# Third layer's experts: all sorted rows kept in SBUF, each tile's outputs scattered from GpSimd into per-token places, plain loads at the end, rank matmuls moved ahead of the projections

## The reference

```python
xn = _layernorm(x, axis=-1)
x = x + _L2_attn_ref(xn, ...) + _L2_ffn_ref(xn, ...)

def _L2_ffn_ref(hidden_states, Wg, W1, W2, W3, bias):      # E = 8, TOP_K = 2, FFN = 128
    x = hidden_states.reshape(-1, hidden_dim)
    routing_weights = jax.nn.sigmoid(x @ Wg.T)
    scores = routing_weights + bias
    _, top_k_index = jax.lax.top_k(scores, TOP_K)
    top_k_weights = jnp.take_along_axis(routing_weights, top_k_index, axis=1)
    top_k_weights = top_k_weights / top_k_weights.sum(axis=-1, keepdims=True)
    expert_w = jnp.einsum('tk,tke->te', top_k_weights, one_hot)
    g = jax.nn.silu(x W1[e]) * (x W3[e]) * expert_w[..., e]
    out = sum over e of g W2[e]
```

## Time and profile before

| | |
|---|---|
| median of 3 runs | 2058.43 us (2058.09 to 2062.5) |
| the profiled execution | 2054.93 us, of which the span is 2053.1 us |
| third layer, from its normalization to its last addition | 656.5 to 806.4 us of the span |
| its loop over 23 tiles of experts | 729.4 to 779.1 us |
| TensorE busy over the span | 90% |
| VectorE, ScalarE, GpSimd busy | 63%, 48%, 52% |

### The profile page before, as it was taken

The page is one execution under the profiler, slowest core; times in us unless marked ns, Lnnn a source line. Parts: engine busy times, 40 slices in busy tenths (PEclk is TensorE's granted clock), DMA queues, the critical chain, the costliest instruction groups (busy, mean ns, idle before and its releaser), DMA issues.

```text
span 2053.1 us, 45861 instructions
## 1 busy us (share of the span) xinstructions
PE 1850.3 (90%) x16855; PEld 1191.3 (58%) x16855; DVE 1287.1 (63%) x2490; ACT 995.4 (48%) x2433; POOL 1072.0 (52%) x2252
## 2 busy tenths in 40 slices
PE   7799997867898885898999999999999999999987
PEld 5422664422244453445677777777777777677766
DVE  2544564685577422535777777777777777777753
ACT  2375232215321341434566656655665666566653
POOL 0521222323100302033888888887888878888873
PEclk7899999989999796899999999999999999999999
DMA  6044422200001333101222222222222222222221
GB/s 155 1 121 148 109 46 56 72 34 1 20 25 26 96 106 95 34 19 40 53 55 61 55 52 63 63 54 53 63 63 54 53 58 63 53 53 62 44 53 33
DMA packets 229260, 121.36 MB, mean 59 GB/s; under 512 B 141712, under 2 KB 208816, under 8 KB 228784
## 3 DMA queue, kind: packets, MB, share of 16 engines
q1 hardware_dynamic: 223424, 109.06, 21.3%
q0 software_dynamic: 5616, 9.38, 2.2%
HBM read 84.88 MB, written 36.68 MB: 59 GB/s over the span
## 4 chain that ended last, share of the span: by engine, by line
PE 22%; POOL 20%; issue 6%; SPq 3%; DVE 3%; DMA 3%; ACT 2%; POOLq 0%; DVEq 0%; ACTq 0%
POOL a_term L2594 8%; POOL a_z L2598 8%; PE ps L2046 5%; PE ps L2056 3%; PE ps L2245 3%; SPq L1979 2%; POOL a_rstd L2570 2%; POOL a_xnorm L2576 2%; DMA a_l<-a_v_dram 2%; PE ps L2276 2%; SPq L1987 1%; DVE a_v L2653 1%; PE ps L2212 1%; PE ps L2286 1%; PE ps L2221 1%
## 5 line engine op out<-in xcount | busy, mean ns | idle before, releaser
L2594 POOL TENSOR_TENSOR a_term<-a_z,a_l 32x14 f32<-32x14 f32 (+6 forms) x896 | 342.1, 382 | 70.3
L2598 POOL TENSOR_TENSOR a_z<-a_z,a_term 32x14 f32<-32x14 f32 (+6 forms) x896 | 341.7, 381 | 70.2
L2624 DVE SCALAR_TENSOR_TENSOR a_qkv<-a_raw,a_taps,a_qkv 128x1024 f32<-128x1024 f32 x192 | 247.0, 1286 | 6.1
L2046 PE MATMUL ps<-all_xn,a_w_qkv 128*128 128x512 f32 x512 | 246.9, 608 | 0.0
L388 POOL DMA_INDIRECT f_rows<-a_row,a_slots x32 | 35.7, 1116 | 192.1 <-DVE a_of_tile L377 146.7
L2245 PE MATMUL ps<-a_out_t,a_w_out 128*128 128x256 f32 x512 | 129.1, 395 | 1.9 <-ACT a_out_t L2468 1.7
L2046 PEld LDWEIGHTS ps<-all_xn,a_w_qkv 128*128 128x128 f32 x512 | 89.1, 193 | 69.3 <-issue 67.5
L2389 ACT ACTIVATE a_raw<-ps 128x512 f32<-128x512 f32 x128 | 76.3, 598 | 108.7 <-PE ps L2046 108.0
L2056 PE MATMUL ps<-a_w_z,all_xn 128*128 128x256 f32 x512 | 122.6, 383 | 0.0
L849 POOL DMA_INDIRECT f_sums<-a_y,a_xs x23 | 36.0, 1566 | 136.5 <-ACT a_y L798 133.5
L2588 POOL COPY a_z<-a_l 32x256 f32<-32x256 f32 x64 | 27.4, 429 | 152.3 <-DMA a_l<-a_v_dram 152.0
(11 more groups left out here) (331 smaller groups left out, 4303.7 us busy)
## 6 DMA issues: line engine op xcount, KB each, us to landing
a_gc_rows<-a_g_dram SPq DMA_DIRECT2D x64, 256.0 KB, 4.7
a_v_dram<-a_v SPq DMA_DIRECT2D x64, 256.0 KB
a_w<-in_f_w SPq DMA_DIRECT2D x24, 512.0 KB, 4.5
a_w_qkv<-in_a_w SPq DMA_DIRECT2D x16, 512.0 KB, 3.8
a_t_dram<-a_z SPq DMA_DIRECT2D x512, 8.0 KB
a_xs<-f_rows SPq DMA_DIRECT2D x46, 130.0 KB, 2.2
a_w_z<-in_a_w SPq DMA_DIRECT2D x16, 256.0 KB, 2.8
a_w_out<-in_a_wo SPq DMA_DIRECT2D x16, 256.0 KB, 3.1
```

The source lines that it names most:

```text
L2046: mm = pe.matmul(ps[:, to, :], w_qkv[:, k, mt * P:(mt + 1) * P], xn[:, k, b * T:(b + 1) * T], start=k == 0, stop=k == KC - 1)
L2594: pool.tensor_tensor(term[:, 0:j, j + 1:], z[:, 0:j, j:j + 1].broadcast_to([HP, j, n]), rows[:, j:j + 1, j + 1:].broadcast_to([HP, j, n]), ...
L2598: pool.tensor_tensor(z[:, 0:j, j + 1:], z[:, 0:j, j + 1:], term[:, 0:j, j + 1:], ALU.add).then_inc(sub_step, 1)
L2624: dve.scalar_tensor_tensor(to, rows, tap, to, ALU.mult, ALU.add).then_inc(conv_ready if j == TAPS - 1 else conv_step, 1)
```

## The change

- All 23 tiles of sorted rows get a place in SBUF (`xs` has `SLOT_TILES` tiles in place of 6). SP loads them in 8 groups right after the scatter, with no wait on the loop.
- The third layer has its own DRAM tensor of rows, which SP fills with blank rows at the end of the loads that it issues in the normalization block. A blank row ends in a place number of its own, past those of the tokens.
- A row ends in its place, `k * N + token`, for the token's choice k. When a tile's `y` is ready GpSimd scatters it with a plain indirect DMA to these places. `y` is a ring of 6 tiles, and ScalarE waits, before it writes a tile again, for that tile's scatter to have landed.
- The stores of `y` by SP and the 16 gathers of GpSimd are gone. SP waits for all scatters and loads the sums with 8 plain DMAs of 256 KB each.
- The rank matmuls stand ahead of the projections.

```diff
@@ class Routing
-    def __init__(self, nc, s, whole, d, name, by_sigmoid, rows=None):
-        self.taken_over = rows is not None
-        self.rows = rows if self.taken_over else nc.dram_tensor(name + "_rows", (SLOT_TILES * P, ROW), F32).ap()
-        self.sums = None if self.taken_over else nc.dram_tensor(name + "_sums", (N + P, C), F32).ap()
+    def __init__(self, nc, s, whole, d, name, by_sigmoid, apart):
+        self.places = TOP * N if apart else N
+        self.rows = nc.dram_tensor(name + "_rows", (SLOT_TILES * P, ROW), F32).ap()
+        self.sums = nc.dram_tensor(name + "_sums", (self.places + (SLOT_TILES if apart else 1) * P, C), F32).ap()
@@ load_rest
-            sp.dma_start(self.row[:, k, :, C + 1:], d["token"]).then_inc(self.r_loaded, 16)
+            sp.dma_start(self.row[:, k, :, C + 1:], d["token"][k if self.apart else 0]).then_inc(self.r_loaded, 16)
@@ fill
+        rows = self.rows.rearrange("(i p) w -> p i w", p=P)
+        if self.apart:
+            sp.dma_start(rows, self.d["blank_apart"]).then_inc(self.filled, 16)
+            return
@@ scatter
-            if not self.taken_over:
-                pool.wait_ge(self.filled, 2 * 16)
+            pool.wait_ge(self.filled, 16 if self.apart else 2 * 16)
@@ linear_and_experts, load
             sp.dma_start(bo[:, :], d["a2_bo"]).then_inc(loaded, 16)
+            route.fill(sp)
@@ buffers
-        XS, DEEP = 6, 3
-        xs, xt = s.buf("xs", [P, XS, ROW]), s.buf("xt", [P, DEEP, KC, P])
+        DEEP, YS = 3, 6
+        xs, xt = s.buf("xs", [P, SLOT_TILES, ROW]), s.buf("xt", [P, DEEP, KC, P])
+        GROUPS = ((0, 1), (1, 2), (2, 4), (4, 7), (7, 11), (11, 15), (15, 19), (19, SLOT_TILES))
-        y, got = s.buf("y", [P, 4, C]), s.buf("got", [P, TOP, TT, C])
+        y, got = s.buf("y", [P, YS, C]), s.buf("got", [P, TOP, TT, C])
@@ SP
                 sp.wait_ge(route.scattered, 16 * TOP * TT)
-                for i in range(XS):
-                    load_rows(i)
-                for i in range(TILES):
-                    store(i)
-                    if i + XS < TILES:
-                        load_rows(i + XS)
+                for n, (a, z) in enumerate(GROUPS):
+                    sp.dma_start(xs[:, a:z, :], route.rows[a * P:z * P, :].rearrange("(i p) w -> p i w", p=P)
+                                 ).then_inc(xs_loaded[n], 16)
+                for v in range(YS):
+                    sp.wait_ge(y_put[v], 16 * ((TILES - 1 - v) // YS + 1))
+                for pair in range(TT // 2):
+                    for k in range(TOP):
+                        first = k * N + 2 * pair * P
+                        sp.dma_start(got[:, k, 2 * pair:2 * pair + 2, :], route.sums[first:first + 2 * P, :].rearrange(
+                            "(t p) c -> p t c", p=P)).then_inc(got_loaded[pair], 16)
@@ TensorE
                     route.turn_rows(pe, ps, ROW_BANK + p % 2, xn, ident, p)
+                route.ranks(pe, ps, ROUTE_BANK)
                 pe.wait_ge(loaded, 4 * 16)
                 for t in range(NT):
...
-                    if t == 3:
-                        route.ranks(pe, ps, ROUTE_BANK)
@@ ScalarE, take_y
-                    if i >= 4:
-                        act.wait_ge(y_stored[i % 4], 16 * (i // 4))
-                    act.activation(y[:, i % 4, :], ps[:, Y[i % 2], 0:C], ACT.Copy,
-                                   scale=xs[:, i % XS, C:C + 1]).then_inc(y_ready, 1)
+                    if i >= YS:
+                        act.wait_ge(y_put[i % YS], 16 * (i // YS))
+                    act.activation(y[:, i % YS, :], ps[:, Y[i % 2], 0:C], ACT.Copy,
+                                   scale=xs[:, i, C:C + 1]).then_inc(y_ready, 1)
@@ GpSimd
-                for v in range(4):
-                    pool.wait_ge(y_stored[v], 16 * ((TILES - 1 - v) // 4 + 1))
-                for tt in range(TT):
-                    for k in range(TOP):
-                        pool.indirect_dma_start(got[:, k, tt, :], None, y_dram, bass.IndirectOffsetOnAxis(
-                            route.slots[:, k, tt:tt + 1], 0)).then_inc(got_loaded[tt // 2], 16)
+                for i in range(TILES):
+                    pool.wait_ge(y_ready, i + 1)
+                    pool.indirect_dma_start(
+                        route.sums, bass.IndirectOffsetOnAxis(xs[:, i, C + 1:C + 2].bitcast(U32), 0),
+                        y[:, i % YS, :], None).then_inc(y_put[i % YS], 16)
@@ VectorE
-                    dve.wait_ge(got_loaded[pair], 16 * TOP * 2)
+                    dve.wait_ge(got_loaded[pair], 16 * TOP)
```

More of the change, by code:

```diff
@@ L186 @@
 class Routing:
[L190 to L195 removed]
+    def __init__(self, nc, s, whole, d, name, by_sigmoid, apart):
+        self.name, self.d, self.by_sigmoid, self.apart = name, d, by_sigmoid, apart
+        self.places = TOP * N if apart else N
+        self.rows = nc.dram_tensor(name + "_rows", (SLOT_TILES * P, ROW), F32).ap()
+        self.sums = nc.dram_tensor(name + "_sums", (self.places + (SLOT_TILES if apart else 1) * P, C), F32).ap()
         self.wr = s.buf("wr", [P, KC, E_ALL])
@@ L243, in fill @@
     def fill(self, sp):
-        sp.dma_start(self.rows.rearrange("(i p) w -> p i w", p=P),
-                     self.d["blank"].unsqueeze(1).broadcast_to([P, SLOT_TILES, ROW])).then_inc(self.filled, 16)
+        rows = self.rows.rearrange("(i p) w -> p i w", p=P)
+        if self.apart:
+            sp.dma_start(rows, self.d["blank_apart"]).then_inc(self.filled, 16)
+            return
+        sp.dma_start(rows, self.d["blank"].unsqueeze(1).broadcast_to([P, SLOT_TILES, ROW])).then_inc(self.filled, 16)
         sp.dma_start(self.sums.rearrange("(i p) w -> p i w", p=P),
@@ L403, in rope_and_experts @@
     with Stage(nc, "a0") as s:
-        route = Routing(nc, s, whole, d, "f0", False)
-        rows = route.rows
+        route = Routing(nc, s, whole, d, "f0", False, False)
         FF = 512
@@ L1303, in _, with linear_and_experts @@
                                                  ALU.add, ALU.add).then_inc(added, 1)
-def linear_and_experts(nc, whole, ps, d, x, xn, ident, norm, rows):
+def linear_and_experts(nc, whole, ps, d, x, xn, ident, norm):
     with Stage(nc, "a2") as s:
@@ L1313, in linear_and_experts @@
         wo, bias, bo = s.buf("wo", [P, KC, C]), s.buf("bias", [P, 3, KC]), s.buf("bo", [P, KC])
-        route = Routing(nc, s, whole, d, "f2", True, rows)
+        route = Routing(nc, s, whole, d, "f2", True, True)
         FF = 128
@@ L1341, in linear_and_experts @@
             s.sem("ctx_ready"), s.sem("out_ready"), s.sem("added"))
-        xs_loaded = [s.sem(f"xs_loaded{v}") for v in range(XS)]
+        xs_loaded = [s.sem(f"xs_loaded{n}") for n in range(len(GROUPS))]
         xt_psum, xt_ready, h_psum, silu_ready, gated_ready, gt_psum, gt_ready, y_psum, y_ready = (
@@ L1345, in linear_and_experts @@
             s.sem("gt_psum"), s.sem("gt_ready"), s.sem("y_psum"), s.sem("y_ready"))
-        y_stored = [s.sem(f"y_stored{v}") for v in range(4)]
-        got_loaded = [whole.sem(f"f2_got_loaded{pair}") for pair in range(TT // 2)]
+        y_put = [whole.sem(f"f2_y_put{v}") for v in range(YS)]
+        got_loaded = [s.sem(f"got_loaded{pair}") for pair in range(TT // 2)]
         both_added, sum_psum, sums_added = s.sem("both_added"), s.sem("sum_psum"), s.sem("sums_added")
@@ L1418, in turn_x @@
                 def turn_x(i):
-                    pe.wait_ge(xs_loaded[i % XS], 16 * (i // XS + 1))
+                    for n, (a, z) in enumerate(GROUPS):
+                        if i == a:
+                            pe.wait_ge(xs_loaded[n], 16)
                     if i >= 2:
@@ L1422, in turn_x @@
                     for k in range(KC):
-                        mm = pe.transpose(ps[:, XT[i % 2], k * P:(k + 1) * P], xs[:, i % XS, k * P:(k + 1) * P],
+                        mm = pe.transpose(ps[:, XT[i % 2], k * P:(k + 1) * P], xs[:, i, k * P:(k + 1) * P],
                                           ident[:, :])
@@ L2923, in _constants @@
         "tile_no": np.tile(np.arange(SLOT_TILES, dtype=f), (P, 1)),
-        "token": _row_ends(np.arange(N).reshape(TT, P).T),
+        "token": np.stack([_row_ends(k * N + np.arange(N).reshape(TT, P).T) for k in range(TOP)]),
         "blank": np.concatenate([np.zeros((P, C + 1), f), _row_ends(N + np.arange(P))], axis=1),
+        "blank_apart": np.concatenate([np.zeros((P, SLOT_TILES, C + 1), f), _row_ends(
+            TOP * N + np.arange(SLOT_TILES * P).reshape(SLOT_TILES, P).T)], axis=2),
     }
@@ L2998, in build @@
         if "a0" in stages:
-            rows = rope_and_experts(nc, s, ps, d, x, xn, ident, looked_up)
+            rope_and_experts(nc, s, ps, d, x, xn, ident, looked_up)
         def norm(name):
@@ L3009, in build @@
         if "a2" in stages:
-            linear_and_experts(nc, s, ps, d, x, xn, ident, norm("n2"), rows)
+            linear_and_experts(nc, s, ps, d, x, xn, ident, norm("n2"))
         if "a3" in stages:
```

9 lines of the change are left out of this document (removed).

## The result

The changed kernel takes 2030.74 us (median of 4 runs, 2026.41 to 2033.46) against 2058.26 us beside it; the ratio is 0.9863, with a 95% interval of 0.9844 to 0.9882. Forecast were 2030.8 us. The total agrees better than its parts do, so the layer has to be taken apart.

The account below looks back on a forecast made before the run. Bounds: TensorE's wait for sorted rows, the loop's 2.19 us pace on a six-tile ring, and a 27.26 us end. Start 3.8, loop 10.3 and end 13.5 sum to 27.6 us off 2058.43: 2030.8 us, range 2025 to 2036.

Parts of the forecast that it names:

- Ranks first: Layer start: rank matmuls ahead of projections bring `place` and first scatter 7.3 us earlier, tile 0's transposes only 2.8 us.
- The clock: Layer start: without an idle stretch TensorE keeps 2.4 GHz through transposes and output matmuls, gaining 1.0 us.
- Resident rows: Third layer's loop: no load hangs on it, outputs come every 1.62 us in place of 2.19, gaining 10.3 us.
- Rival C: Loop keeps its old pace, the first two outputs showing only TensorE's saved-up lead: 2041.1 us, chance 0.07.
- The scatter beside the loop: GpSimd's 23 `y` scatters take 0.97 us plus 0.30 pause, 1.27 a tile against 1.62, so they hide at no cost.
- rivals A and B: Loop scatters: GpSimd becomes the bound at 1.86 us a tile (chance 0.10), or VectorE shuts it out at 2.27 (0.05).
- The end: Last `y` to last addition: 8 plain loads replace the gathers, 13.8 us in place of 27.26, gaining 13.5.
- the bound of 10.8 from 247 GB/s: Final loads' pessimistic case: 2.10 MB at 247 GB/s plus 2.3 us, 10.8 us in place of 7.9, gain 10.6.
- The estimate of 6.8 us: Final loads by the Trainium skill's DMA fit, 2.0 us plus bytes over 436 GB/s; gain 1.1 us larger.
- Blank rows: Start: SP's 2990 KB fill lands by 682.1, before the first scatter at 689.4; costs nothing, at worst 5 us.
- rival D: Loop: VectorE slows GpSimd's scatters past 2.80 us each, the ring fills, kernel slower, 2062 us; chance 0.03.
- rival E: Fourth layer gives the gains back, or the change is within 0.2%: 2058 us, chance 0.02.

Follow-up runs that it names:

- the resident rows alone: Kernel before with only all 23 row tiles resident, loaded in 8 groups; SP's stores, gathers and the ranks' place kept: layer 141.46 us, ratio 0.9945.
- double the load: Changed kernel with every output scatter issued twice, first into a spare tensor nobody reads: layer 156.14 us, one execution 2056.2 us.

## Why the prediction was right, and where it was not

- **Ranks first: right.** `place` was forecast 7.3 us earlier and came 7.5 us earlier in the layer (28.78 against 36.32); the scatter took 23.7 us where 24.1 were kept. That most of this is not gained, because `put_out(0, ·)` is late next, held too: it begins 58.39 us into the layer, before 58.44. The 0.2 us that I charged for the ranks at half the clock were nothing.
- **The clock: right, too small.** 1.0 us was forecast for keeping 2.4 GHz; from the transposes to the first tile's matmul are 3.88 us in place of 5.36, so 1.5. With the wait itself, 3.19 in place of 2.8, the start gave 4.67 in place of 3.8.
- **Resident rows: right.** 10.63 us against 10.3, from a pace read off two outputs. That loads and not stores held it is shown by the resident rows alone. Rival C is out, since the pace of 1.62 us held to the 19th output.
- **The scatter beside the loop: right.** 0.967 us, and 0.66 us idle a tile; rivals A and B are out, also at double the load. The choice of the earlier trace rows over the earlier trace rows carried this. Only the first layer's form with add takes 1.56 us; that the add is the reason follows from the form alone and was not tried.
- **The end: shorter as forecast, but by another path and less.** 17.5 us against 13.8. Eight plain loads did replace the gathers, but the forecast let the last pair's landing decide, and what decided was pair 1's landing and the chain behind it. Three terms make up the 3.7 us.
  - The last two outputs are ready almost together, and the last scatter, queued behind the one before at 1.27 us, starts 1.2 us after the last output and not 0.3: 0.9 us.
  - Pair 1 was added 7.2 us after the first issue, where 3.4 + 1.5 = 4.9 had been read from the earlier trace rows: 2.3 us. That 1.5 was the distance between the landings of two loads that overlap, and I used it as the price of each further 512 KB of a longer row of loads. It was short for the last landing too, 9.9 us where 7.9 were forecast; that lies inside the bound of 10.8 from 247 GB/s. But the gain, 9.7 us, is below the 10.6 of that bound, since the bound had the same path. The estimate of 6.8 us that the prediction set beside this term was further off than its own 7.9.
  - From pair 1's addition to the end VectorE and TensorE need 6.54 us, while I let the last pair decide, with 3.0 us from pair 1 to it and 3.02 behind it: 0.5 us. The old gathers had hidden that chain, as each pair came 5 us after the one before.
- **Blank rows: right.** Landed at 678.9, the scatter starts 3.83 us after `place`, as before (3.80). The first tile's matmul is at 68.61 us of the layer, and at 68.58 and 68.57 in the two kernels with early ranks and no fill.
- **Slower, rival D: not met, but priced wrong.** Its deciding point was put at 2.80 us a tile. At 2.54 the layer is already 6.3 us longer than before. Of its length 9 us are the gaps, whose cause is open, and from the last scatter's start to the end are 16.1 us where 13.5 were forecast.
- **Given back by the fourth layer, rival E:** out, as far as one profile of each kernel tells: outside the layer the span is 1.0 us shorter, not longer.
- **The total.** The layer gave 25.05 us, not 27.6, and the median moved by 27.5 between runs that differ by several us outside the layer. The forecast's own range of 2025 to 2036 holds either; that the medians agree to 0.1 us is chance.

## What to carry to other kernels

Read a ring's pace from its first turns, which run on what was loaded ahead: where they are faster than the rest, suspect the ring and not an engine. Here the difference times the turns was the gain, 10.3 us forecast and 10.6 measured, and a kernel with only the ring removed showed it. For a group of loads, ask which landing lets the longest dependent chain start, because later ones may be hidden behind that chain; and do not take the distance between two overlapping landings for a rate. Work on an idle engine is free only below the pace of its neighbours: here 1.27 us of 1.62 cost nothing, and 2.54 cost the layer 31 us, more than the whole change had gained.

## What the runs showed of the hardware

- Plain indirect scatters from GpSimd beside VectorE's gate and copy, which read PSUM, stayed at 963 to 972 ns in 23 and in 46 of them; six of the 16 in the changed kernel's row scatter took between 1.36 and 1.93 us, each beside VectorE work with two inputs in SBUF, while others beside such work stayed at 0.97 or 0.98. The Trainium skill's SBUF — State Buffer, section Who interferes with whom, says that a VectorE instruction with two SBUF inputs contends with a GpSimd instruction that reads SBUF, and one with a single SBUF input, outside the two-port modes, does not. The trace agrees with both. The same section takes it, as inferred, that such a two-input operation does not hold up the writing of descriptors, which the prediction left out; the indirect DMAs here also read their offsets from SBUF, and no run separates the two.
- An idle stretch of 3 to 4 us on TensorE cost more than itself: eight matmuls of 512 columns took 3.60 us where the granted clock stayed at 1.00, and 4.62 and 5.78 us after a wait of 3.02 and 4.16, where it fell to 0.50.
- 1 MB of plain loads issued within the first microsecond had landed after about 5 us; the same MB as four of eight loads in a row took 6.3 to 7.2 us. All 2.1 MB had landed after 7.9 to 8.9 us in the first case and 9.0 to 9.9 us in the second.
- With GpSimd sending 46 indirect DMAs, most of them 0.30 us after the one before, about 9 of 66 us went into gaps of the other engines that the trace gives no releaser for.
